# The residual kept by features, and per-row factors spread through DRAM

## The reference

```python
# front ("attention"), per sequence
y = conv3(x, w_dw) @ w_pw.T;  x = x + y
q, k, v = split(x @ w_qkv.T)                  # 16 heads of 8
q, k = elu(rope(q)) + 1, elu(rope(k)) + 1
num   = q . cumsum(k v^T);  denom = q . cumsum(k)
attn  = (num / (denom + 1e-06)) @ w_o.T
gate  = sigmoid((x - shifted(x)) @ w_gate.T + b_gate)
x = x + gate * attn
h = layernorm(x) * ln_g + ln_b
gw = softmax(h @ w_moe_gate.T)                # 4 experts, all used
# mixture
ffn = sum_e gw[e] * (silu(h @ w1[e].T + b1[e]) @ w2[e].T + b2[e])
out = x + ffn                                 # then a layer of routed experts
```

## Time and profile before

| what | us |
|---|---|
| median of 3 runs (1468.48 to 1475.07) | 1471.02 |
| the profiled execution | 1480.5 |
| its span, first to last instruction | 1478.7 |
| `attention_front` ends, `mixture` begins | 454 |
| scatter of the last rows, end of `mixture` | 895 |

### The profile page before, as it was taken

The page is one execution under the profiler, slowest core; times in us unless marked ns, Lnnn a source line. Parts: engine busy times, 40 slices in busy tenths (PEclk is TensorE's granted clock), DMA queues, the critical chain, the costliest instruction groups (busy, mean ns, idle before and its releaser), DMA issues. The chain is left out here.

```text
span 1478.7 us, 33273 instructions
## 1 busy us (share of the span) xinstructions
PE 1266.4 (86%) x10164; PEld 984.0 (67%) x10164; DVE 1013.0 (69%) x3390; ACT 814.8 (55%) x1703; POOL 712.6 (48%) x907
## 2 busy tenths in 40 slices
PE   2899999999986999999999965883988888739998
PEld 1566767676655877777777754773666666539997
DVE  3588888888735899999999984764566666522222
ACT  2355555556426776767777643552556555525554
POOL 3355565656420234343443542335566676426666
PEclk9799999999877999999999986996999999859999
DMA  1101011110102321212112205674111112168872
GB/s 62 40 30 39 31 33 33 31 37 28 45 13 62 69 54 44 64 41 62 40 48 59 73 16 142 196 202 146 27 44 47 49 55 44 44 233 300 266 264 69
DMA packets 70844, 117.53 MB, mean 79 GB/s; under 512 B 9746, under 2 KB 36635, under 8 KB 70768
## 3 DMA queue, kind: packets, MB, share of 16 engines
q1 hardware_dynamic: 58736, 93.49, 21.3%
q0 software_dynamic: 9856, 21.52, 4.6%
q10 hardware_dynamic: 2176, 1.61, 0.4%
HBM read 79.35 MB, written 29.88 MB: 74 GB/s over the span
## 5 line engine op out<-in xcount | busy, mean ns | idle before, releaser
L1159 DVE TENSOR_TENSOR m_Sl<-m_S,m_Sh 128x512 fp32r<-128x512 f32 x256 | 195.5, 769 | 23.3 <-ACT m_S L1076 20.6
L1076 ACT ACTIVATE m_S<-PS,W 128x512 f32<-128x512 f32 x256 | 174.7, 690 | 39.0 <-issue 33.1
L1071 ACT ACTIVATE m_Sh<-PS,W 128x512 fp32r<-128x512 f32 x192 | 132.9, 692 | 72.1 <-PE PS L996 64.5
L1459 POOL DMA_INDIRECT rows<-r_row,r_posi x128 | 131.2, 1025 | 36.2 <-issue 36.0
L761 DVE TENSOR_TENSOR am<-PS,C 128x512 f32<-128x512 f32 x192 | 119.6, 678 | 25.9 <-PE PS L454 25.4
L1693 PEld LDWEIGHTS PS<-f_wt,f_hid 128*128 128x128 f32 x960 | 121.3, 194 | 4.4
L1693 PE MATMUL PS<-f_wt,f_hid 128*128 128x128 f32 x960 | 121.5, 277 | 0.0
L1682 PE MATMUL PS<-f_xT,f_wt 128*128 128x256 f32 x480 | 121.2, 390 | 0.0
L965 POOL TENSOR_TENSOR m_oe<-m_oe 128x512 f32<-128x512 f32 x48 | 67.8, 1412 | 102.2 <-DVE m_oe L1140 101.7
L994 PE MATMUL PS<-m_HH,m_w1h 128*128 128x512 f32 x256 | 107.7, 421 | 7.1 <-DVE m_w1l L1112 4.7
L352 POOL TENSOR_TENSOR am<-am,C 128x512 f32<-128x512 f32 x64 | 81.6, 1275 | 54.8 <-ACT am L636 53.5
(11 more groups left out here) (237 smaller groups left out, 3127.2 us busy)
## 6 DMA issues: line engine op xcount, KB each, us to landing
f_wt<-wr SPq DMA_DIRECT2D x40, 578.0 KB
f_row<-rows SPq DMA_DIRECT2D x40, 260.0 KB
f_wt<-wr SPq DMA_DIRECT2D x40, 256.0 KB, 2.8
m_gb<-gates SPq DMA_DIRECT2D x8, 1024.0 KB, 7.7
m_raw<-gates SPq DMA_DIRECT2D x8, 1024.0 KB, 7.9
f_row<-rows SPq DMA_DIRECT2D x40, 132.0 KB, 2.1
mid<-f_res SPq DMA_DIRECT2D x20, 256.0 KB, 3.3
X<-x SPq DMA_DIRECT2D x16, 256.0 KB, 2.8
```

Of the source, the lines that this page charges most:

```text
L1071: nc.scalar.activation(Sh[:, n % 4, :], PS[:, n % 3, :], ACT.Silu, bias=w("b1")[:, n:n + 1]).then_inc(sh_ready, 1)
L1076: nc.scalar.activation(S[:, n % 3, :], PS[:, n % 3, :], ACT.Silu, bias=w("b1")[:, n:n + 1]).then_inc(s_ready, 1)
L1159: nc.vector.tensor_tensor(Sl[:, n % 4, :], S[:, n % 3, :], Sh[:, n % 4, :].bitcast(F32), ALU.subtract).then_inc(sl_ready, 1)
L1459: nc.gpsimd.indirect_dma_start(out=self.rows, out_offset=bass.IndirectOffsetOnAxis(ap=self.posi[:, u, t:t + 1], axis=0), in_=self.row[:, u ...
```

## The change

- The residual is kept by features. A second input xt, the transpose of x, is loaded into X (seen as XT, features on partitions) behind each load of x, which now goes into H's place for that sequence. `residual2` adds x2T to XT without a transpose. In the mixture GpSimd adds XT to the weighted sum (`sums`, e == 1), so that `back` turns the finished output, and ScalarE copies it to X (`copy_back`); VectorE's `residual` goes.
- The second normalisation works by features too. x2 is still turned for the statistics. ScalarE keeps a copy of x2 by features (`keep_x2`), writes the 512 scales and shifts to DRAM and reads them back spread over all partitions (`spread_scale2_out`, `spread_scale2_in`: 4 KB, then 512 KB), and GpSimd multiplies and adds one step later (`scale_z`, `shift_z`). `scale_h` and the logits move to that later step (a new phase e_ = c_ - 1), so `turn_z` and `normalise2` go, except for the last sequence, which keeps the old way.
- The denominators are turned while small (`turn_den`, one transpose), written to DRAM and read back with each head's row eight times (32 KB, then 256 KB).
- The router's scores are taken from `back`'s source by features with a router centred beforehand (`centre` times `router0`), and scaled by the deviation in `dve_largest`; `pe_turn` and `act_copy_xT` go from the mixture. The normalised rows are still made for the scatter.
- `ROUNDED = ()`: ScalarE writes Sh in every chunk.

The core of the diff:

```diff
+            steps(None, 0, 0, None, None, None)
+            steps(None, 1, 1, 0, None, None)
+            steps(0, 0, 2, 1, None, None)
+            steps(1, 1, 3, 2, 0, None)
+            steps(2, 0, 4, 3, 1, 0)
+            steps(3, 1, 5, 4, 2, 1)
+            with eng.Fori(0, (BATCHES - 6) // 2) as i:
                 for u in range(2):
-                    b = i * 2 + (2 + u)
-                    steps(b, u, b + 2, b + 1, b + (-1))
-            steps(BATCHES - 2, 0, None, BATCHES - 1, BATCHES - 3)
-            steps(BATCHES - 1, 1, None, None, BATCHES - 2)
-            steps(None, 0, None, None, BATCHES - 1)
+                    b = i * 2 + (4 + u)
+                    steps(b, u, b + 2, b + 1, b + (-1), b + (-2))
+            steps(BATCHES - 2, 0, None, BATCHES - 1, BATCHES - 3, BATCHES - 4)
+            steps(BATCHES - 1, 1, None, None, BATCHES - 2, BATCHES - 3)
+            steps(None, 0, None, None, BATCHES - 1, BATCHES - 2)
...
-                sp.dma_start(X[:, bass.ds(b * CT, CT), :], src).then_inc(x_in, 16)
+                sp.dma_start(columns(H, b).rearrange("p (c d) -> p c d", c=CT), src).then_inc(x_in, 16)
+                sp.dma_start(columns(XT, b), xt[:, bass.ds(b * SEQ, SEQ)]).then_inc(xt_in, 16)
...
+            def scale_z(b):
+                pool.wait_ge(x2_copied, b + 1)
+                pool.wait_ge(sb2_in, 16 * b + 16)
+                nc.gpsimd.tensor_tensor(x2c[:, :], x2c[:, :], sb2[:, 0, :], ALU.mult).then_inc(scaled, 1)
+            def shift_z(b):
+                pool.wait_ge(scaled, b + 1)
+                nc.gpsimd.tensor_tensor(x2c[:, :], x2c[:, :], sb2[:, 1, :], ALU.add).then_inc(z_ready, 1)
...
                     mask_last(b, 0)
+                if e_ is not None:
+                    scale_z(e_)
+                if b is not None:
                     keep_x1(b, u)
                     mask_last(b, 1)
+                if e_ is not None:
+                    shift_z(e_)
                 if c_ is not None:
-                    inverse_deviation(c_, ln2_stats, mv2, ve2, ve2_done, rstd2, rstd2_ready, shift2, shift2_ready, z_ready, negated2)
+                    inverse_deviation(c_, ln2_stats, mv2, ve2, ve2_done, scale2[:, 0, :], rstd2_ready, scale2[:, 1, :], shift2_ready, scale2_out, negated2, 16)
...
-            def turn_spread(b):
-                pe.wait_ge(spread_ready, b + 1)
-                after_previous(pe, lg_ready, b)
-                for t in range(CT):
-                    mm = nc.tensor.transpose(PS[:, 7, t * P:(t + 1) * P], spread[:, t * P:(t + 1) * P], ident)
-                mm.then_inc(rdT_psum, 1)
+            def turn_den(b, c_):
+                pe.wait_ge(den_step, 2 * b + 2)
+                if c_ is not None:
+                    pe.wait_ge(ln2, CT * c_ + CT)
+                nc.tensor.transpose(PS[:, 7, 0:P], den[:, :, :].rearrange("p a n -> p (a n)"), ident).then_inc(denT_psum, 1)
             def gate(b, u):
-                pe.wait_ge(rdT_ready, b + 1)
+                if since(b, 2):
+                    pe.wait_ge(lg_ready, b + (-1))
+                pe.wait_ge(denT_ready, b + 1)
...
+                    tokens = x2T[:, t * P:(t + 1) * P] if final(b) else x2T[:, :].rearrange("d (p t) -> d t p", t=CT)[:, t, :]
...
-            def logits(b):
+            def logits(b, c_, d):
                 pe.wait_ge(H_ready, b + 1)
+                bank = 0 if final(c_) and not final(b) else 7
+                if c_ is not None:
+                    pe.wait_ge(ln2, CT * c_ + CT)
+                if d is not None:
+                    pe.wait_ge(denT_ready, d + 1)
                 for t in range(CT):
-                    mm = nc.tensor.matmul(PS[:, 7, t * MOE:(t + 1) * MOE], h[:, t * P:(t + 1) * P], w("moe_gate"),
+                    mm = nc.tensor.matmul(PS[:, bank, t * MOE:(t + 1) * MOE], h[:, t * P:(t + 1) * P], w("moe_gate"),
...
+                if b is not None:
+                    turn_den(b, c_)
...
-                if c_ is not None:
-                    turn_z(c_)
+                if e_ is not None:
+                    logits(e_, c_, b)
                 if n is not None:
                     project(n, u, "q", 0)
-                if c_ is not None:
-                    logits(c_)
+                if final(c_):
+                    turn_z(c_)
+                    logits(c_, None, None)
                 if b is not None:
                     weigh(b, u, 3)
-                    turn_spread(b)
                 if n is not None:
                     project(n, u, "k", 1)
...
-            def normalise2(b):
+            def keep_x2(b):
+                act.wait_ge(x2_step, 2 * b + 2)
+                after_previous(act, H_ready, b)
+                nc.scalar.activation(x2c[:, :], x2T[:, :], ACT.Copy).then_inc(x2_copied, 1)
+            def spread_scale2_out(b):
                 act.wait_ge(shift2_ready, b + 1)
-                act.wait_ge(x_added, b + 1)
-                after_previous(act, lg_psum, b)
+                after_previous(act, sb2_in, b, 16)
+                act.dma_start(z_dram.rearrange("s (p t) -> p s t", p=P), scale2[:, :, :]).then_inc(scale2_out, 16)
+            def spread_scale2_in(b):
+                act.wait_ge(scale2_out, 16 * b + 16)
+                after_previous(act, z_ready, b)
+                act.dma_start(sb2[:, :, :], z_dram.unsqueeze(0).to_broadcast([P, 2, SEQ])).then_inc(sb2_in, 16)
+            def normalise_last():
+                act.wait_ge(shift2_ready, BATCHES)
+                act.wait_ge(lg_psum, BATCHES - 1)
                 for t in range(CT):
                     ins = nc.scalar.activation(z[:, t, :], PS[:, 7, t * P:(t + 1) * P], ACT.Identity,
-                                               bias=shift2[:, t:t + 1], scale=rstd2[:, t:t + 1])
-                ins.then_inc(z_ready, 1)
...
-            def spread_out(b):
-                act.wait_ge(den_step, 2 * b + 2)
-                nc.scalar.activation(spread[:, :].rearrange("p (h m) -> p h m", m=HD),
-                                     den[:, 1, :].unsqueeze(2).to_broadcast([P, CT * HEADS, HD]),
-                                     ACT.Copy).then_inc(spread_ready, 1)
-            def copy_rdT(b):
-                act.wait_ge(rdT_psum, b + 1)
-                nc.scalar.activation(rdT[:, :], PS[:, 7, :], ACT.Copy).then_inc(rdT_ready, 1)
+            def copy_den(b):
+                act.wait_ge(denT_psum, b + 1)
+                after_previous(act, den_out, b, 16)
+                nc.scalar.activation(denT[:, :], PS[:, 7, 0:P], ACT.Copy).then_inc(denT_ready, 1)
+            def spread_den_out(b):
+                act.wait_ge(denT_ready, b + 1)
+                after_previous(act, rdT_in, b, 16)
+                act.dma_start(den_dram.rearrange("h t p -> (h t) p"), denT[CT * HEADS:, :]).then_inc(den_out, 16)
+            def spread_den_in(b):
+                act.wait_ge(den_out, 16 * b + 16)
+                after_previous(act, wo_psum, b)
+                src = den_dram.rearrange("h t p -> h (t p)").unsqueeze(1).to_broadcast([HEADS, HD, SEQ])
+                act.dma_start(rdT[:, :], src).then_inc(rdT_in, 16)
             def gate_tanh(b):
                 act.wait_ge(gate_psum, b + 1)
+                after_previous(act, x2_psum, b)
+                after_previous(act, x_added, b)
                 nc.scalar.activation(th[:, :], PS[:, 7, :], ACT.Tanh, bias=w("b_gate"), scale=0.5).then_inc(th_ready, 1)
...
             def scale_h(b):
-                act.wait_ge(zT_psum, b + 1)
-                nc.scalar.activation(h[:, :], PS[:, 7, :], ACT.Identity, bias=w("ln_b"), scale=w("ln_g")).then_inc(h_ready, 1)
-                nc.scalar.activation(H[:, bass.ds(b * SEQ, SEQ)], PS[:, 7, :], ACT.Identity, bias=w("ln_b"),
+                act.wait_ge(z_ready, b + 1)
+                after_previous(act, lg_psum, b)
+                nc.scalar.activation(h[:, :], x2c[:, :], ACT.Identity, bias=w("ln_b"), scale=w("ln_g"))
+                nc.scalar.activation(columns(H, b), x2c[:, :], ACT.Identity, bias=w("ln_b"), scale=w("ln_g")).then_inc(H_ready, 1)
...
+                if e_ is not None:
+                    scale_h(e_)
+                if c_ is not None and not final(c_):
+                    keep_x2(c_)
                 if b is not None:
-                    spread_out(b)
                     raw_scores(b, 2)
+                    copy_den(b)
+                    spread_den_out(b)
+                if c_ is not None and not final(c_):
+                    spread_scale2_out(c_)
                 if n is not None:
                     copy_x1(n, u)
-                if c_ is not None:
-                    normalise2(c_)
-                    scale_h(c_)
+                if b is not None:
+                    spread_den_in(b)
+                if c_ is not None and not final(c_):
+                    spread_scale2_in(c_)
                 if b is not None:
                     raw_scores(b, 3)
-                if c_ is not None:
-                    copy_logits(c_)
```

(48 more changed lines are left out.)

114 lines of the change are left out of this document (69 added, 45 removed).

## The result

The kernel after takes 1482.02 us (median of 20 runs) where the kernel before takes 1474.04 (20 runs): ratio 1.0051, 95% interval 1.0027 to 1.0074. The forecast was 1455, some 16 us faster; by the ratio it is 7.5 us slower. (One of the 20 executions of the kernel after took 1601 us at a granted clock of 0.76; the ratio leaves it out, the median doesn't.) The profiled execution took 1481.3 us, its span 1479.5, nearly the same as the one of before (1480.5, 1478.7). That near equality hides two unlike stages that the change touches and a third that differs without it. The first rows are the first operation of the mixture, from VectorE of the kernel after in order of time, and the scatter of the mixture's last rows, from GpSimd; before, these stood at 454.18 and 894.26.

A forecast was written before the change was run, and what follows sets the result against it. Attention was taken as bound by a loop through qphi, SP's copies and x's load, the mixture by PE. Terms +13 + 0.3 - 8 - 17 - 4 = -15.7 us gave a median of 1455 us, range 1434 to 1478.

The forecast's parts named there:

- The forecast of 25.0 us a step: Attention loop: 23.3 + 1.2 + 0.3 + 0.2 us against 23.9 before, +1.1 a step, +13 us over 12 steps.
- 2.91 + 1.2: Attention loop, issue of x's load to first statistics: 2.91 us before, plus 1.2 for x at half rate beside the broadcasts.
- 9.09 + 0.2: Attention loop, statistics to end of qphi: 9.09 us without the wait of `divide`, plus 0.2 for GpSimd slowing VectorE.
- a rival of its own, priced at 1 us a step: Attention: PE waits more, its clock stays longer at 1.2 GHz; 1 us a step, 1467 us, chance 0.12.
- the slower rival: Attention: delays of x and of SP's issues at upper bounds, 26.9 us a step, 1478 us; chance 0.14.
- The floor of 23.3: Attention loop from qphi through SP's copies and x's load to the next qphi: 23.3 us without the wait of `divide`.
- the credit of 0.6 us a step for the wait of `divide`: Attention loop: the 0.69 us wait for spread denominators goes, so the loop is 0.6 below today's 23.9.
- the four transposes with their wait go: -1.26: Mixture step: PE's transposes of normalised rows (0.42 us) and their wait for VectorE (0.84) go, -1.26 us a step.
- VectorE being late; -0.5: Mixture step: PE's wait for Sl shrinks as VectorE loses four casts and the residual, -0.5 us a step.
- charged with 0.6: Mixture step: ScalarE writes Sh before the last S, delaying the next batch's first `up`, +0.6 us a step.
- the -21 us: Whole mixture: -1.2 us a step for 14 batches (-17), and -4 at the end of the stage.
- The end of attention: -8 forecast: Last attention steps: waits behind the transposes of z (2.2 us) and of the denominators (1.8) go, twice, -8 us.

The follow-up runs named there:

- e3: The kernel after, with SP's loads of x and xt issued one step earlier; ratio 0.9857 to the kernel before.
- e4: The kernel after, with GpSimd's multiplication of z moved behind the copy of x1 and the second mask; ratio 1.0059 to the kernel before.
- e6: The kernel before, with SP's loads of x issued one step earlier; ratio 0.9971 to the kernel before.
- e7: The kernel before, with ROUNDED empty (no casts by VectorE, ScalarE writes Sh in every chunk) and nothing else; ratio 0.9937 to the kernel before.
- e8: The kernel after, with VectorE's casts of every fourth Sh back (ROUNDED = (3,)); ratio 1.0196 to the kernel before.
- e9: The kernel before with three edits: x loaded one step earlier, no casts by VectorE, a fourth PSUM bank; ratio 0.9828 to the kernel before.
- e5: The kernel after, unchanged, run again on the chip of several follow-up runs as their base; ratio 1.0062 to the kernel before.
- e2: The kernel after, with the load of xt issued by ScalarE some 10 us ahead of the load of x; ratio 1.0072 to the kernel before.
- e12: The kernel before, with two added broadcasts from DRAM (256 KB and 512 KB) by ScalarE that nothing reads; ratio 1.0205 to the kernel before.

## Why the prediction was wrong

**The steps of the attention stage: right mechanism, sized at half.** The forecast of 25.0 us a step was 26.0 in the middle steps; over all twelve (from the load of x at 65.8 to the last one 315.9 us, before from 66.3 288.9) it was +27 us and not +13. By its terms, in the step above: to the issue of x 11.26 + 0.3, measured 11.1; from there to the statistics 2.91 + 1.2, measured 4.30, so the delay of x was 1.4 and well sized; from the statistics to the end of qphi 9.09 + 0.2, measured 10.4. The term that failed is the last. The fall of PE's clock behind the gap that the late x makes costs 1.2 us there (9.14 us in the steps without it, 10.36 with it): the wait of `state` for PE, and a qphi that starts beside GpSimd's multiplication. It stood only in a rival of its own, priced at 1 us a step, as if it were another case and not what follows from the forecast's own delay. The 0.2 for GpSimd was right where the clock holds (e3) and is 0.7 where it has fallen; e4 shows that moving the multiplication wins nothing. As the text said itself, the slower rival decides from 2.4 us a step on; measured were 2.1 above before.

**The floor of 23.3: wrong, though harmless to the result.** "That is the number to keep in mind" was put together from two steps: the wait of 0.51 for x is of one, the wait of 0.69 of `divide` of the other (`divide` waited 0.16 in the step that waited for x). e6 takes the load out of the loop and the step stays at 23.9. No run gives back the credit of 0.6 us a step for the wait of `divide`; in e6 VectorE waits for PE and for the denominators at the same pace. e3 shows what the spared transposes are worth once nothing is late: 23.7 against 23.9.

**The mixture: the step that failed is "the four transposes with their wait go: -1.26".** I put the wait of 0.84 us down to the transposes, since it stood ahead of them, and the one for Sl to "VectorE being late; -0.5". Both were VectorE being late, and e7 shows that taking its casts is enough: the transposes stay, and the step loses 1.0 us. The change of ROUNDED, which the sum credited with part of 0.5 us and charged with 0.6, is the whole gain of the mixture; the residual by features with GpSimd's addition, credited with most, costs 0.2 us a step (e7 against after), or 0.9 where VectorE has the casts to do (e8). Why VectorE is late at the transposes without casts once PE is on time (e9) stays open. Of the -21 us -7.7 came: the first sequences, which the sum didn't price, took 5.2 us more (91.0 against 85.9 from the first operation to the fifth load of gates), the twelve steps from there on -10.1 (12 x 0.84; the forecast had 1.2 for each of 14), and the end -2.9 in place of -4.

**The end of attention: -8 forecast, -5.7 measured** (from the last load of x to the mixture 93.2 us against 98.9), and -3.8 between e5 and e7.

Together: 27 where 13 stood, -5.7 where -8 stood, -7.7 where -21 stood; the start, put at +0.3, came out at -0.6. The loss by the transfers was foreseen as the forecast's largest cost; the gain set against it wasn't the change's.

## What to carry to other kernels

A wait in front of an instruction belongs to the engine that ends it, not to the instruction: before a removal is credited with it, ask what made that engine late, and who is next to wait for it. A transfer that is added where a load on the critical path is issued is paid as the delay, and again if the gap that the delay makes lowers PE's clock ahead of work on the path (1.4 and 1.2 us in the kernel after). Here loading one step ahead was worth 2% on the kernel after and 0.3% on the kernel before. And a chain that fits the period isn't yet what sets it: take it away before you count on its floor.

## What the runs showed of the hardware

- A load of 256 KB lands after 2.8 us in the kernel before. It takes 4.1 with a broadcast of 256 KB issued up to 0.6 us ahead of it, one of 512 KB up to 0.8 us behind and a load of 256 KB behind it on its own queue; 3.8 with that last load moved away (e2, where the broadcasts stay); and 5.2 with both broadcasts issued 1.6 to 2 us ahead (e12).
- PE's clock was at 1.2 GHz behind a gap of 2.9 us in the kernel after and behind one of 2.2 in e12, though not in every step of e12: at 293 it stayed at 2.4. It fell in e3 too, in steps whose gaps are each 1.1 us or less: a mean of 0.93 over two steps, with 0.96 in the kernel before.
- What a fall of the clock costs depends on where it comes: 1.2 us ahead of qphi in the kernel after, 0.3 there in e12, nothing that shows in e3, where it comes behind the denominators.
- The same softmax attention took 224.3, 213.3 and 195.0 us from its first to its last normalised row in three executions (before, after, e5), with granted clocks of 0.93, 0.98 and 0.97; the clock doesn't order them. And the chips differ: on one the kernel before takes 1448 us, on another 1475.
- VectorE's operations with two SBUF inputs took longer with a GpSimd operation beside them: qphi 0.7 to 1.8 us, the scan 1.2 to 1.6 (means), two subtractions 1.3 to 3.1.
